# The deformable gather as one stream of quads, with VectorE's product over four PSUM banks

## The reference, cut to what matters

```python
def _deform(x, ow, ob):
    off = _conv(x, ow, 1) + ob[None, :, None, None]        # two offsets per channel and pixel
    off = off.reshape(B, C, 2, H, W)
    py = jnp.clip(yy + off[:, :, 0], 0.0, H - 1)
    px = jnp.clip(xx + off[:, :, 1], 0.0, W - 1)
    ...                                                    # floor, neighbours, weights wy and wx
    return v00 * (1 - wy) * (1 - wx) + v01 * (1 - wy) * wx + v10 * wy * (1 - wx) + v11 * wy * wx

h = _bn(_conv(_deform(x, ow1, ob1), w1, 0), ...)           # 256 channels sampled, 64 out
h = _bn(_conv(_deform(h, ow2, ob2), w2, 1), ...)           # 64 channels sampled
h = _bn(_conv(_deform(h, ow3, ob3), w3, 0), ...)           # 64 channels sampled, 256 out
```

## Time and profile before

| | |
|---|---|
| median of three runs | 5976.82 us |
| the profiled execution, own time | 5969.8 us |
| its span, first to last instruction | 5968.1 us |
| TensorE busy | 4860.9 us, 81% |
| VectorE busy | 3608.7 us, 60% |
| ScalarE busy | 1857.1 us, 31% |
| GpSimd busy | 1478.1 us, 25% |
| DMA queue of SyncE, share of 16 engines | 37.7% |
| mean granted TensorE clock | 0.887 of full speed |

### The profile page before, as it was taken

One profiled execution on the slowest core, in us unless ns is written; L12 is line 12 of the kernel. 1 busy time (PEld: TensorE's weight loads), 2 busy tenths in 40 slices (PEclk: granted clock), 3 DMA queues, 4 the chain that ended last, 5 costly groups with the idle time before them and its releaser, 6 DMA issues. The chain is left out here.

```text
span 5968.1 us, 82574 instructions
## 1 busy us (share of the span) xinstructions
PE 4860.9 (81%) x30592; PEld 2689.8 (45%) x30592; DVE 3608.7 (60%) x4317; ACT 1857.1 (31%) x2899; POOL 1478.1 (25%) x1828
## 2 busy tenths in 40 slices
PE   4787887876999799979989994959596983985886
PEld 2333333324777677757767771313131332332222
DVE  6888888875666566652212223848484873863764
ACT  2222222202222122220000003848484751751660
POOL 0222222220000000011101002636363651642540
PEclk7888888867999899989999996979797996997988
DMA  1000000001000000011111119989898968978962
GB/s 30 15 20 17 21 22 21 15 21 65 15 15 8 22 15 15 8 61 74 43 71 74 53 67 193 217 180 218 178 220 181 217 171 183 218 145 143 221 178 91
DMA packets 377577, 558.13 MB, mean 94 GB/s; under 512 B 167464, under 2 KB 169064, under 8 KB 376264
## 3 DMA queue, kind: packets, MB, share of 16 engines
q1 hardware_dynamic: 377160, 552.64, 37.7%
HBM read 439.27 MB, written 113.25 MB: 93 GB/s over the span
## 5 line engine op out<-in xcount | busy, mean ns | idle before, releaser
L1415 POOL TENSOR_SCALAR g_kw<-g_kw 128x512 f32<-128x512 f32 x1536 | 960.8, 650 | 936.7 <-ACT g_kw L1401 637.1
L1401 ACT ACTIVATE g_vw<-ps,l_index 128x512 f32<-128x512 f32 x1536 | 971.0, 686 | 520.4 <-PE ps L1457 520.1
L1434 DVE SCALAR_TENSOR_TENSOR g_prod<-g_vw,ps 128x1024 f32<-128x1024 f32 x768 | 903.3, 1218 | 213.0 <-PE ps L1472 213.0
L1294 PE MATMUL ps<-o_pad,o_ow 128*128 128x512 f32 x3456 | 852.5, 409 | 8.5 <-DVE o_pad L822 7.7
L1457 PE MATMUL ps<-g_coord,l_spread 128*128 128x512 f32 x1920 | 678.5, 452 | 147.6 <-DMA g_coord<-coords 147.4
L1093 PE MATMUL ps<-l_pair,l_w 128*128 128x512 f32 x3072 | 780.3, 403 | 0.0
L1294 PEld LDWEIGHTS ps<-o_pad,o_ow 128*128 128x128 f32 x3456 | 657.3, 191 | 198.0 <-DVE o_pad L822 7.9
L1472 PE MATMUL ps<-g_kw,g_img 32*32 32x512 f32 x12288 | 458.9, 620 | 311.7 <-DVE g_prod L1434 272.5
L1457 PEld LDWEIGHTS ps<-g_coord,l_spread 128*128 128x128 f32 x1920 | 313.1, 194 | 831.1 <-ACT g_vw L1401 615.6
L1093 PEld LDWEIGHTS ps<-l_pair,l_w 128*128 128x128 f32 x3072 | 575.6, 191 | 156.6 <-issue 29.4
L1423 DVE TENSOR_SCALAR g_kw<-g_rows,l_index 128x1536 f32<-128x1536 f32 x384 | 389.8, 1015 | 416.0 <-DMA g_rows<-whole 416.0
(11 more groups left out here) (247 smaller groups left out, 4911.9 us busy)
## 6 DMA issues: line engine op xcount, KB each, us to landing
g_rows<-whole SPq DMA_DIRECT2D x1536, 192.0 KB, 4.4
g_coord<-coords SPq DMA_DIRECT2D x96, 512.0 KB, 7.2
coords<-o_parts SPq DMA_DIRECT2D x32, 1024.0 KB, 4.0
l_x<-xcur SPq DMA_DIRECT2D x16, 1024.0 KB, 6.5
coords<-o_parts SPq DMA_DIRECT2D x32, 512.0 KB, 5.1
g_img<-dense SPq DMA_DIRECT2D x96, 128.0 KB, 8.6
gathered<-g_res SPq DMA_DIRECT2D x48, 256.0 KB, 4.8
l_xn<-in_x SPq DMA_DIRECT2D x8, 1024.0 KB, 5.0
```

The source lines that it names most:

```text
L1294: ins = nc.tensor.matmul(ps[:, lo:lo + HALF], ow[:, a, kk, tap, y, k * P:(k + 1) * P], padded_rows(pad[:, m, c, kk], j, tap), start=(n == ...
L1401: nc.scalar.activation(to, bank(a % RING), ACT.Relu, bias=index[:, 0:1]).then_inc(sem("ring_read"), 1)
L1415: nc.gpsimd.tensor_scalar(part, part, 1.0, 0.0, ALU.min, ALU.max).then_inc(sem("clamped"), 1)
L1434: nc.vector.scalar_tensor_tensor(prod[:, n % PB, 2 * half:2 * half + 2, :].rearrange("p r n -> p (r n)"), vw[:, n % VB, 2 * half:2 * half ...
```

## The change

It rewrites `build_gather` and the layout of what it reads.

1. **No turns.** The loop of turns is gone: each gather is one unrolled stream of all its quads (256, 64, 64) in one block. Coordinates and images have two buffers instead of four, and those of set s + 1 are issued among the row copies of set s, at its quads 7 to 11. Addresses are constants instead of registers.
2. **Row copies.** `whole` is laid out by half image, so that three neighbouring channels are one run of 6 KB, and one DMA per quad replaces four.
3. **Images.** `dense` is laid out line by line, so a load is one DMA in runs of 4 KB instead of four in runs of 128 bytes; the stores in the offset stages now have runs of 128 bytes.
4. **Coordinates.** The tile has 80 partitions instead of 128: the column positions of all four channels, the row positions of channel 0 alone; two DMAs. The selector shrinks with it.
5. **Product.** One instruction over four PSUM banks replaces two.

```diff
 def send_rows(q):
-    src = whole[bass.ds(n0 + s, 1), :, j * HALF:(j + 1) * HALF]\
-        .rearrange("a (r t q) n -> t (a r) q n", r=4, t=QUADS)[g]
-    for r in range(4):
-        sp.dma_start(rows[r * SIDE:(r + 1) * SIDE, q % SB],
-                     src[r, OWN:4].partition_broadcast(SIDE)).then_inc(sem(f"rows_sent{q % SB}"), 16)
+    src = whole[s, j].rearrange("(r t q) n -> t r q n", r=4, t=QUADS)[g, :, 1:4].rearrange("r q n -> r (q n)")
+    sp.dma_start(rows[:, q % SB].rearrange("p c n -> p (c n)"),
+                 src.unsqueeze(1).to_broadcast([4, SIDE, 3 * HALF])).then_inc(sem(f"rows_sent{q % SB}"), 16)
...
+def load_image(s):
+    if s >= 2:
+        sp.wait_ge(sem("rows_summed"), PER_SET * (s - 1))
+    sp.dma_start(img[:, s % 2].rearrange("p g c j -> p (g c j)"),
+                 dense[s].rearrange("i (r g) j -> r i (g j)", r=4)).then_inc(sem(f"img_loaded{s % 2}"), 16)
+
+def load_coords(s, t):
+    at_x = coords[s, 1].rearrange("s (r t q) n -> t s r q n", r=4, t=4)[t]
+    at_y = coords[s, 0].rearrange("s (r t h q) n -> t q s r h n", r=4, t=4, h=2)[t, 0]
+    sp.dma_start(coord[0:CM, s % 2, t, :].bitcast(F32), at_x).then_inc(sem(f"coord_loaded{s % 2}{t}"), 16)
+    sp.dma_start(coord[CM:CROWS, s % 2, t, :].bitcast(F32), at_y).then_inc(sem(f"coord_loaded{s % 2}{t}"), 16)
...
 for q in range(SB, Q):
     send_rows(q)
+    s, part = divmod(q, PER_SET)
+    if s + 1 < sets:
+        if part == 7:
+            load_image(s + 1)
+        if 8 <= part < 12:
+            load_coords(s + 1, part - 8)
     if q % QUADS == SB + 2 and q >= QUADS:
         store(q // QUADS - 1)
...
-def weigh(n, half):
+def weigh(n):
...
-    nc.vector.scalar_tensor_tensor(prod[:, n % PB, 2 * half:2 * half + 2, :].rearrange("p r n -> p (r n)"),
-                                   vw[:, n % VB, 2 * half:2 * half + 2, :].rearrange("p r n -> p (r n)"),
-                                   1.0, ps[:, lo:lo + 2 * HALF], ALU.min,
-                                   ALU.mult).then_inc(sem("weighted"), 1)
+    nc.vector.scalar_tensor_tensor(prod[:, n % PB].rearrange("p r n -> p (r n)"),
+                                   vw[:, n % VB].rearrange("p r n -> p (r n)"),
+                                   1.0, ps[:, ROW_BANK * HALF:(ROW_BANK + 4) * HALF], ALU.min,
+                                   ALU.mult).then_inc(sem("weighted"), 1)
...
-dense = dram("dense", (B * C, N))
+dense = dram("dense", (B * C // P, SIDE, P, SIDE))
-whole = dram("whole", (B * C // P, P, N))
+whole = dram("whole", (B * C // P, NH, P, HALF))
```

In the first offset stage the store of an image to `dense` becomes two DMAs (one per 128 channels), and the reload of the buffer waits for both:

```diff
-sp.dma_start(dense[bass.ds((b0 + m) * C, C), :].rearrange("(k p) n -> p k n", p=P),
-             x[:, m % 2]).then_inc(sem(f"stored{m}"), 16)
+for kk in range(KC):
+    sp.dma_start(dense[bass.ds((b0 + m) * KC + kk, 1)].rearrange("a i p j -> (a p) i j"),
+                 x[:, m % 2, kk, :].rearrange("p (i j) -> p i j", j=SIDE))\
+      .then_inc(sem(f"stored{m}"), 16)
 if m + 2 < IMGS:
-    sp.wait_ge(sem(f"stored{m}"), 16)
+    sp.wait_ge(sem(f"stored{m}"), 16 * KC)
```

More of the change, by code:

```diff
@@ L1298, in build_offsets_1, with build_gather @@
             st.clear()
-def build_gather(nc, ps, consts, dense, coords, whole, gathered, blocks, tag):
+def build_gather(nc, ps, consts, dense, coords, whole, gathered, sets, tag):
     with ExitStack() as ctx:
@@ L1315, in build_gather @@
         res = st.sb("res", [P, 2, HALF])
-        rows = st.sb("rows", [P, SB, SENT, HALF])
-        quads = [(s, j, g) for s in range(SETS) for j in range(NH) for g in range(QUADS)]
-        Q = len(quads)
+        rows = st.sb("rows", [P, SB, 3, HALF])
+        quads = [(s, j, g) for s in range(sets) for j in range(NH) for g in range(QUADS)]
+        Q, PER_SET = len(quads), NH * QUADS
         bank = lambda i: ps[:, i * HALF:(i + 1) * HALF]
@@ new lines, in build_gather, with _, send_rows, store @@
+        with nc.Block() as block:
+            @block.sync
+            def _(sp):
+                def send_rows(q):
+                    s, j, g = quads[q]
+                    if q >= SB:
+                        sp.wait_ge(sem("sent_relu"), q - SB + 1)
+                    src = whole[s, j].rearrange("(r t q) n -> t r q n", r=4, t=QUADS)[g, :, 1:4].rearrange("r q n -> r (q n)")
[11 more added lines that the diff above has]
+                    sp.dma_start(coord[CM:CROWS, s % 2, t, :].bitcast(F32), at_y).then_inc(sem(f"coord_loaded{s % 2}{t}"), 16)
+                def store(r):
+                    s, j = divmod(r, NH)
+                    sp.wait_ge(sem("res_ready"), r + 1)
+                    sp.dma_start(gathered[s * P:(s + 1) * P, j * HALF:(j + 1) * HALF],
+                                 res[:, r % 2, :]).then_inc(sem(f"stored{r % 2}"), 16)
+                send_rows(0)
+                load_coords(0, 0)
+                load_image(0)
+                send_rows(1)
+                send_rows(2)
+                for t in range(1, 4):
+                    load_coords(0, t)
+                for q in range(SB, Q):
+                    send_rows(q)
+                    s, part = divmod(q, PER_SET)
[4 more added lines that the diff above has]
+                            load_coords(s + 1, part - 8)
+                    if q % QUADS == SB + 2 and q >= QUADS:
+                        store(q // QUADS - 1)
+                store(sets * NH - 1)
+                for r in range(2):
+                    sp.wait_ge(sem(f"stored{r}"), 16 * sets)
+            @block.scalar
+            def _(act):
+                def evacuate(r):
+                    act.wait_ge(sem("folded"), QUADS * (r + 1))
+                    if r >= 2:
+                        act.wait_ge(sem(f"stored{r % 2}"), 16 * (r // 2))
+                    nc.scalar.activation(res[:, r % 2, :], bank(FOLD_BANK), ACT.Copy).then_inc(sem("res_ready"), 1)
+                for n in range(-2, Q):
+                    for task in turn_tasks(n):
@@ L1461, in rows_step @@
-                    def rows_step(n):
-                        s, j, g = quads[n]
-                        if j == 0 and g == 0:
-                            pe.wait_ge(sem(f"img_loaded{s}"), 64)
-                        pe.wait_ge(sem("clamped"), 4 * (n + 1))
-                        if n:
-                            pe.wait_ge(sem("weighted"), 2 * n)
-                        for c in range(4):
-                            for r in range(4):
-                                mine = slice(r * SIDE, (r + 1) * SIDE)
-                                lo = (ROW_BANK + r) * HALF
-                                ins = nc.tensor.matmul(ps[c * SIDE:(c + 1) * SIDE, lo:lo + HALF], img[mine, s, g, c, :],
-                                                       kw[mine, n % KB, c, :], start=True, stop=True)
-                        ins.then_inc(sem("rows_summed"), 1)
@@ new lines, in _ @@
+                    if n >= QUADS and n % QUADS == 0:
+                        evacuate(n // QUADS - 1)
+                evacuate(sets * NH - 1)
+            @block.gpsimd
+            def _(pool):
+                for q in range(Q):
+                    for c in range(4):
+                        if c == 0:
+                            pool.wait_ge(sem("ring_read"), at["k", q, 0] + 1)
+                        else:
+                            pool.wait_ge(sem("sent_relu"), q + 1)
+                        part = kw[:, q % KB, c, :]
+                        nc.gpsimd.tensor_scalar(part, part, 1.0, 0.0, ALU.min, ALU.max).then_inc(sem("clamped"), 1)
```

243 lines of the change are left out of this document (98 added, 145 removed).

## The result

The changed kernel takes 7410.38 us, the median of four runs (7397.39 to 7427.6), against 5976.25 us (5971.12 to 5979.78) for the kernel before on the same chip. The ratio is 1.240, with a 95% interval of 1.2375 to 1.243: 24% slower. The forecast was 7370.

A forecast was written before the change was run, and what follows sets the result against it. It took the PSUM ring of VectorE and TensorE to bound settled gather quads, with DMA close behind. Rest 4080 + copies 3206 + starts and ends 54 + stores 24 = 7364 us of span, forecast 7370 us, range 7150 to 9300.

The forecast's parts named there:

- The row copy on four engines: Gathers: the merged row copy, with four outermost pieces, runs on four DMA engines, always the same, instead of 16.
- Rival A: Gathers: the row copy spreads over all engines, 4.26 us per quad, faster than before; chance 0.08.
- 26.0 GB/s for one busy engine: Gather copies: rate of each of the four engines, taken from the offset weights' load in 6 KB runs.
- Rival B: Gathers: four engines at the crowded 13.7 GB/s, 253 us per set, 10,230 us in all; chance near this bound 0.1.
- 133.6 us per set, 8.35 per quad: Gathers: time for 3.473 MB per engine and set at 26.0 GB/s; 24 sets take 3206 us.
- starts and ends: Gathers: first row instruction 5.7 us after first issue, plus the end after the last; 18 us, three times, 54 us.
- The stores in small runs, 24 us: Last two offset stages: stores in 128-byte runs delay the last store of each of four turns, 24 us.
- The product, 2272 ns: VectorE in the gathers: one 2048-column instruction replaces a 2.35 us pair, 31 us if the ring bounds; costed at nothing.
- the ring: Settled gather quads: VectorE and TensorE take turns on the same four PSUM banks, 3.81 us per quad before.
- The clock at 0.5 and hidden: TensorE in the gathers: clock falls from 1.0 to 0.5, 16 matmuls take 2.02 us, ring 4.6 us, under 8.35.
- The price of rival A, 5590 to 5795 us: Whole kernel if all engines share the row copy: 5795 us at 219 GB/s, 5590 if the ring bounds; chance 0.08.
- The turns go, 350 us: Gathers: six cold starts lose 425 us; all but three would go, saving about 350 us if copies kept up.

The follow-up runs named there:

- two-engine run: The changed kernel with a quad's row copy as two copies of 64 partitions, each source with 2 as outermost count; 10,263.11 us.
- fifth experiment: The first experiment with the image load as four copies of 32 partitions; 5922.98 us, ratio 0.9903 to the kernel before.
- first experiment: The changed kernel with a quad's row copy again as four copies of 32 partitions, in 6 KB runs; 6062.86 us, ratio 1.0166 to the kernel before.
- tenth experiment: The seventh with a coordinate load every second quad (8, 10, 12, 14); 5692.05 us, ratio 0.9527 to the kernel before.
- eighth experiment: The seventh with the four row copies in block order 0, 1, 2, 3 again; 5786.67 us, ratio 0.968 to the kernel before.
- ninth experiment: The changed kernel with the image load alone as four copies over 16 engines; 7348.38 us, ratio 1.2286 to the kernel before.
- sixth experiment: The first experiment with the four row copies issued in block order 0, 2, 1, 3; 5982.23 us, ratio 1.0022 to the kernel before.
- seventh: The fifth and sixth experiments together, plus the old coordinate load (128 partitions, 16 outer pieces); 5728.44 us, ratio 0.958 to the kernel before.

## Why the prediction was right, step by step

- **The row copy on four engines: right.** Waits in all 384 quads, a share of 0.28, the loss of 1348 us that goes when the copy is cut as before, and the two-engine run at twice the quad time all agree. Rival A, all engines share it, would have shown quads under 4.3 us; they take 7.5. That two such copies use the same engines is what the two-engine run adds.
- **26.0 GB/s for one busy engine: right,** 26.3 measured. It came from a stage with quite other work, with the run length of 6 KB in common. Rival B, engines that slow one another, is out: no settled quad shows it with four engines. With 16 it is real, 14.4 to 15.2 GB/s per busy engine in the order 0, 1, 2, 3.
- **133.6 us per set, 8.35 per quad: right within 2%.** The three gathers ran 2192.1, 556.1 (5939.0 to 6495.1) and 564.6 us (6649.6 to 7214.2), 3313 us against 3206 + 54 = 3260. Settled quads were right, 7.47 us against 7.56 by the prediction's rate. From their first to their last row instruction the three gathers take 3231 us, so 25 of the missing 53 us lie in the quads with side loads. The other 28 lie in the starts and ends, 82 us in place of 54: the first row copy too is on four engines, and the first row instruction comes 12.2 us after its issue, not 5.7:

```profile
3616.79 0.64 SPq L1342 DMA_DIRECT2D g_rows<-whole  x1
...
3628.95 1.02 DVE L1427 TENSOR_SCALAR g_kw<-g_rows,l_index 128x1536 f32<-128x1536 f32 x1 [13.24 <-DMA g_rows<-whole]
```

- **The stores in small runs, 24 us: wrong, they cost nothing.** From the last store of the first gather to the first row copy of the second, over the offset stage between, it is 134.8 us (5804.22 to 5939.01) against 135.2 before (4869.45 to 5004.64), and all that lies outside the gathers takes 7395.4 - 3313 = 4082 us against 4080. By luck the 24 us made good a part of the 53 missing, so the total came out nearer (0.5%) than its terms.
- **The product, 2272 ns: right,** 2280 measured, and hidden, as costed. Its gain if the ring bounds was put at 31 us and is 19, since the ring went to 3.75 and not 3.73 us.
- **The clock at 0.5 and hidden: right, but what it costs was sized too low.** TensorE's 16 matmuls take 2.02 us instead of 1.15:

```profile
4404.31 2.02 PE L1473 MATMUL ps<-g_kw,g_img 32*32 32x512 f32 x32 [3.40 <-DVE g_prod L1436]
```

The prediction put the ring at this clock at 4.6 us and left out that TensorE's other matmuls slow down too. The fifth experiment shows 6.53 us, with TensorE busy throughout. And TensorE did not idle for over half of a quad, but for a quarter (74.76 of 100 us busy). Under quads of 7.47 us even 6.53 stays hidden, so the total did not suffer.
- **The price of rival A, 5590 to 5795 us: wrong.** It took the row copy as the only one on few engines, and a set's bytes as spread evenly. The first experiment is that case, at 6063 us: the image and coordinate loads use four and eight engines, and every row copy behind them waits for the most loaded engine. I had counted them on those engines in my own sum, and not in the rival's. The rival's sum also lacks the quads of 6.53 us at the lower clock, 21 in the first experiment's trace.
- **"The turns go, 350 us":** not seen in the changed kernel, since the copies did not keep up. In the tenth experiment, where they nearly do, 283 us are gained (5975.45 - 5692.05), some 19 of them by the product.

The 136 us of the eighth experiment's coordinate load come out as two parts. The engine that carries most has 49,152 + 40,960 bytes in a coordinate quad with eight engines and 49,152 + 32,768 with 16, which at 14.9 GB/s is 0.5 us per quad, 46 us over the 84 coordinate loads issued beside row copies. The quads of 6.53 us, 86 us in the fifth experiment's trace, are gone in the eighth's. That trace is of the fifth's slowest run, though, so the second part is an upper end.

What stays open: why TensorE stays at the lower clock for some stretches and not for others, and what slows the quad in the ninth experiment in which the image copies are issued.

## What to carry to other kernels

Count the outermost pieces of both sides of each copy before merging copies: one large broadcast of four sources ran on four engines, and four small ones on sixteen, for the same bytes. A low DMA share beside a long wait for a DMA is the sign of it, not a sign of spare bandwidth that helps. Look at small side loads too: a copy on all engines is only as fast as the engine that has most queued in front of it, so 24 loads of 512 KB on four engines cost 140 us more than the same loads on sixteen. And a stall can cost more than itself, by the quads at the lower clock that follow.

## What I had not expected of the hardware

- Copies with few pieces do not spread over the engines by turns: two copies of two pieces each ran on one pair (15 us, not 7.5).
- The order in which four copies of 32 partitions are issued changes the rate of a busy engine: from 15.2 to 16.4 GB/s between the first and the sixth experiment, from 14.6 to 15.6 between the eighth and the seventh.
- A stall in the copies can leave TensorE at the lower clock after they have caught up. Then TensorE bounds the quads at 6.53 us instead of 3.75 though it is busy all the time, in the fifth experiment for up to five such quads in a row, before it is back at the higher clock.
- A VectorE instruction over four PSUM banks costs less than two over two banks each (2.28 to 2.29 against 2.35 us), and each further 512 columns cost what the earlier trace rows say.
- The profile gives no landing time for the row, image and coordinate copies of the changed kernel. It gives one for the image as soon as that is cut in four (4.9 us in the fifth experiment), and one for the coordinates as soon as they have 16 outer pieces (11.9 us in the seventh).
